# A decoder layer with a product-key FFN: maxima and indices of the next step taken in the middle of a step, and the gather of the indices moved to GpSimd

## The reference, cut to what matters

```python
q = jnp.einsum('bnd,de->bne', x, w_q)                      # 2 x 8 heads x 128
q = (q - mean) * rsqrt(var + BN_EPS) * bn_gamma + bn_beta  # over all 1600 tokens
sim = jnp.einsum('pbnhd,hkpd->pbnhk', q, keys)             # 2 halves x 8 heads x 32 keys
sx, ix = top_k(sim[0], 8);  sy, iy = top_k(sim[1], 8)
all_scores  = sx[..., :, None] + sy[..., None, :]          # 64 per head
all_indices = ix[..., :, None] * 32 + iy[..., None, :]
scores, pk = top_k(all_scores, 8)
indices = take_along_axis(all_indices, pk, axis=-1)        # 64 experts of 1024 per token
h = softmax(scores) * gelu_new(einsum('bnd,bnhkd->bnhk', x, down_embed[indices]))
out = einsum('bnhk,bnhkd->bnd', h, up_embed[indices])
```

## Time and profile before

| | before |
|---|---|
| median of three runs | 1294.25 us |
| the profiled execution | 1297.17 us |
| its span, first to last instruction | 1295.5 us |
| FFN, within that span | from about 1001 us to the end |
| VectorE busy over the span | 1139.7 us, 88% |
| GpSimd busy over the span | 622.4 us, 48% |
| mean granted TensorE clock | 0.91 of full speed |

### The profile page before, as it was taken

How to read it: one execution, slowest core, us unless ns; L and a number is a source line. 1 busy time by engine, 2 the same in 40 slices (tenths; PEclk the granted TensorE clock), 3 DMA queues, 4 the chain that set the end, 5 groups by cost and what they waited for, 6 DMA issues and landing times. The chain is left out here.

```text
span 1295.5 us, 32702 instructions
## 1 busy us (share of the span) xinstructions
PE 1163.4 (90%) x12758; PEld 908.5 (70%) x12762; DVE 1139.7 (88%) x2858; ACT 885.1 (68%) x1248; POOL 622.4 (48%) x520
## 2 busy tenths in 40 slices
PE   6969999999999999999999999999997748888878
PEld 4746777777767777776777777677776628778778
DVE  7768899999989999898999989998986679999984
ACT  4768888888888888888988888898874332222111
POOL 3226667757566775756677575767240300000000
PEclk9779999999999999999999999999998765667666
DMA  8119999999999999999999999998996300000000
GB/s 176 25 47 206 195 193 197 199 183 191 200 206 200 191 203 184 191 206 194 212 184 203 186 196 203 180 186 177 187 188 134 91 1 2 5 6 5 5 5 6
DMA packets 665393, 186.25 MB, mean 144 GB/s; under 512 B 653938, under 2 KB 662294, under 8 KB 664854
## 3 DMA queue, kind: packets, MB, share of 16 engines
q1 hardware_dynamic: 665238, 184.16, 74.7%
HBM read 19.97 MB, written 0.82 MB: 16 GB/s over the span
## 5 line engine op out<-in xcount | busy, mean ns | idle before, releaser
L1174 PE MATMUL ps<-pT,xa_hi 128*128 128x128 f16 x2288 | 380.8, 217 | 20.9 <-ACT uT L1009 20.9
L986 ACT ACTIVATE e<-ps,bias 128x1444 f32<-128x1444 f32 (+1 forms) x208 | 305.8, 1470 | 128.8 <-DVE bias L1058 128.1
L1178 PE MATMUL ps<-pT,xa_hi 128*128 128x128 f16 x2288 | 380.7, 217 | 2.2 <-DMA pT<-p 2.2
L1175 PE MATMUL ps<-pT,xa_lo 128*128 128x128 f16 x2288 | 380.8, 217 | 0.0
L1056 DVE TENSOR_REDUCE nmax<-ps 128x1 f32<-128x1444 f32 (+1 forms) x208 | 343.9, 1653 | 14.1 <-PE ps L1158 13.0
L1068 DVE TENSOR_TENSOR p<-e,p 128x1408 f16<-128x1408 f32 (+3 forms) x288 | 304.4, 1098 | 41.9 <-ACT p L994 41.0
L994 ACT ACTIVATE p<-e 128x1408 f16<-128x1408 f32 (+1 forms) x208 | 288.2, 1385 | 13.9 <-ACT e L986 0.7
L942 POOL TENSOR_TENSOR p<-e,p 128x1408 f16<-128x1408 f32 (+1 forms) x128 | 196.5, 1556 | 181.9 <-ACT p L994 181.9
L1174 PEld LDWEIGHTS ps<-pT,xa_hi 128*128 128x128 f16 x2288 | 222.1, 98 | 48.9 <-issue 36.0
L1156 PE MATMUL ps<-xT_hi,q_hi 128*128 128x512 f16 (+1 forms) x624 | 229.9, 368 | 4.0 <-POOL q_lo L931 3.3
L1175 PEld LDWEIGHTS ps<-pT,xa_lo 128*128 128x128 f16 x2288 | 222.1, 98 | 12.9
(11 more groups left out here) (238 smaller groups left out, 1929.2 us busy)
## 6 DMA issues: line engine op xcount, KB each, us to landing
raw<-in_ctx SPq DMA_DIRECT2D x16, 704.0 KB
pT<-p SPq DMA_TRANSPOSE x416, 3.7
f_wq<-in_L_ffn_w_q SPq DMA_DIRECT2D x1, 1024.0 KB, 5.3
f_wqt<-in_ffn_wq_t SPq DMA_DIRECT2D x2, 512.0 KB, 6.7
raw<-in_ctx SPq DMA_DIRECT2D x48, 18.0 KB
x_tok<-in_x SPq DMA_DIRECT2D x4, 200.0 KB
out_x<-ost SPq DMA_DIRECT2D x6, 128.0 KB, 1.9
wk_t<-in_wk_t SPq DMA_DIRECT2D x1, 512.0 KB, 8.7
```

The costliest lines, as they stand in the source:

```text
L986: act.activation(e32[t % E_BUF][rows, :], score_banks(t)[rows, 0:T], ACT.Exp, bias=bias[rows, t % N_BUF:t % N_BUF + 1]).then_inc(e_done, 1)
L1174: pe.matmul(out, hi, ph, start=n == 0, stop=False)
L1175: pe.matmul(out, lo, ph, start=False, stop=False)
L1178: pe.matmul(out, hi, pl, start=False, stop=False)
```

## The change

It touches only `ffn`.

- The gather's multiply and its three additions leave VectorE. A new function `gathered(i)` does them on GpSimd, with the semaphore `gather` between them. It waits for the mask (`pick`) and for `idxw` (`wide_idx`). VectorE waits for its result (`sel_done`) before `eu`.
- The maxima, the indices and the cast `idxf` of step i+1 are made during step i. All 32 maxima and `AHEAD` = 20 of the 32 `max_index` stand between `sel`'s weights (L1655) and `eu`. The other 12 and the cast stand behind L1674. `EARLY` and its six maxima go.
- `weigh(i - 1, 0)` and `weigh(i - 1, 1)` stood ahead of the maxima of `comb`, `weigh(i - 1, 2)` behind L1629. Now 0 is behind L1629, 1 behind L1655, 2 ahead of the wait for the gather, 3 behind `norm_shift`.
- The three parts of `norm_stats(i - 2)` stand among the maxima and indices of the next step, part 2 behind the 20 indices. `norm_shift(i - 2)` stands behind the cast.
- GpSimd's order in a step becomes `norm_rstd(i - 2)`, `gathered(i)`, `combine(i + 1)`.
- ScalarE's order becomes `picks(i)`, `hidden(i, 0)`, `sims_out(i + 1)`, the exponentials, `hidden(i, 1)`, `last_norm(i - 2)`, then `rT`, `cT`, `w_hi`.

The diff, cut to its core:

```diff
         @block.gpsimd
+            def gathered(i):
+                nh, w = step_shape(i)
+                na = nh * NB
+                pool.wait_ge(pick, 3 * i + 3)
+                pool.wait_ge(wide_idx, i + 1)
+                pool.tensor_tensor(out=eq[...], in0=eq[...], in1=idxw[...], op=ALU.mult).then_inc(gather, 1)
+                pool.wait_ge(gather, 3 * i + 1)
+                pool.tensor_tensor(out=half4[...], in0=eq[0:w, 0:na, 0:4, :], in1=eq[0:w, 0:na, 4:8, :], op=ALU.add).then_inc(gather, 1)
+                pool.wait_ge(gather, 3 * i + 2)
+                pool.tensor_tensor(out=half2[...], in0=half4[0:w, 0:na, 0:2, :], in1=half4[0:w, 0:na, 2:4, :], op=ALU.add).then_inc(gather, 1)
+                pool.wait_ge(gather, 3 * i + 3)
+                pool.tensor_tensor(out=ij[...], in0=half2[0:w, 0:na, 0, :], in1=half2[0:w, 0:na, 1, :],
+                                   op=ALU.add).then_inc(sel_done, 1)
+
+            combine(0)
+            wide_rows(1)
             for i in range(NSTEP):
-                combine(i)
-                if i == 0:
-                    wide_rows(1)
                 if i >= 2:
                     norm_rstd(i - 2)
+                gathered(i)
+                if i + 1 < NSTEP:
+                    combine(i + 1)
         @block.scalar
             for i in range(NSTEP):
+                picks(i)
                 hidden(i, 0)
-                if i >= 2:
-                    last_norm(i - 2)
-                hidden(i, 1)
-                picks(i)
                 if i + 1 < NSTEP:
                     sims_out(i + 1)
                 act.wait_ge(dsc_done, i + 1)
                 act.activation(esc[...], dsc[...], ACT.Exp).then_inc(esc_done, 1)
+                hidden(i, 1)
+                if i >= 2:
+                    last_norm(i - 2)
                 act.wait_ge(selT_ps, i + 1)
         @block.vector, in step(i), behind the weights sel[:, 2]
-                dve.wait_ge(pick, 7 * i + 5)
-                dve.tensor_tensor(out=half4[...], ...)
-                ...
+                if i:
+                    weigh(i - 1, 1)
+                if i >= 2:
+                    norm_stats(i - 2, 0)
+                if i + 1 < NSTEP:
+                    next_maxima(i + 1)
+                if i >= 2:
+                    norm_stats(i - 2, 1)
+                if i + 1 < NSTEP:
+                    next_indices(i + 1, 0)
+                if i >= 2:
+                    norm_stats(i - 2, 2)
+                if i:
+                    weigh(i - 1, 2)
                 dve.wait_ge(sel_done, 4 * i + 1)
                 ...
                 dve.tensor_copy(sel[0:w, 0:2, 0:nh, :], erc[0:w, :, 0:nh, :]).then_inc(sel_done, 1)
+                if i + 1 < NSTEP:
+                    next_indices(i + 1, 1)
+                    next_cast(i + 1)
+                if i >= 2:
+                    norm_shift(i - 2)
                 if i:
                     weigh(i - 1, 3)
```

More of the change, by code:

```diff
@@ L1193 @@
 NSTEP = -(-NT // STEP_TOK)
-EARLY = 6
+AHEAD = 20
 PAD = P + 4
@@ L1277, in ffn @@
         sim_ps, sim_done, top_done, comb_done, best_done = (sem(n) for n in ("sim_ps", "sim_done", "top_done", "comb_done", "best_done"))
+        idxf_done, gather = sem("idxf_done"), sem("gather")
         dsc_done, esc_done, pick, sel_done, selT_ps, selT_done = (sem(n) for n in ("dsc_done", "esc_done", "pick", "sel_done", "selT_ps", "selT_done"))
@@ L1367, in norm_rstd @@
                 pool.tensor_tensor(out=frs[0:w, 0:nh], in0=fve[0:w, 0:nh], in1=nhalf[0:w, 0:nh], op=ALU.pow).then_inc(z_rstd, 1)
+            def gathered(i):
[3 more added lines that the diff above has]
+                pool.wait_ge(wide_idx, i + 1)
+                pool.tensor_tensor(out=eq[0:w, 0:na, :, :], in0=eq[0:w, 0:na, :, :], in1=idxw[0:w, 0:na, :, :], op=ALU.mult).then_inc(gather, 1)
+                pool.wait_ge(gather, 3 * i + 1)
+                pool.tensor_tensor(out=half4[0:w, 0:na, :, :], in0=eq[0:w, 0:na, 0:4, :], in1=eq[0:w, 0:na, 4:8, :], op=ALU.add).then_inc(gather, 1)
+                pool.wait_ge(gather, 3 * i + 2)
+                pool.tensor_tensor(out=half2[0:w, 0:na, :, :], in0=half4[0:w, 0:na, 0:2, :], in1=half4[0:w, 0:na, 2:4, :], op=ALU.add).then_inc(gather, 1)
+                pool.wait_ge(gather, 3 * i + 3)
+                pool.tensor_tensor(out=ij[0:w, 0:nh, :, :].rearrange("s a n k -> s (a n) k"), in0=half2[0:w, 0:na, 0, :], in1=half2[0:w, 0:na, 1, :],
+                                   op=ALU.add).then_inc(sel_done, 1)
+            combine(0)
+            wide_rows(1)
             for i in range(NSTEP):
-                combine(i)
-                if i == 0:
-                    wide_rows(1)
                 if i >= 2:
                     norm_rstd(i - 2)
+                gathered(i)
+                if i + 1 < NSTEP:
+                    combine(i + 1)
             norm_rstd(NSTEP - 2)
@@ L1432, in picks @@
                 nh, w = step_shape(i)
-                act.wait_ge(pick, 7 * i + 1)
+                act.wait_ge(idxf_done, i + 1)
+                if i:
+                    act.wait_ge(gather, 3 * i - 2)
                 act.activation(idxw[0:w, 0:nh * NB, :, :],
@@ L1568, in norm_shift, with next_maxima, next_indices, next_cast @@
                                          op0=ALU.mult, op1=ALU.mult).then_inc(fnm_done, 1)
+            def next_maxima(i):
+                nh, w = step_shape(i)
+                if i:
+                    dve.wait_ge(sim_done, i)
+                    dve.wait_ge(comb_done, i)
+                    dve.wait_ge(top_done, 2 * i)
+                    dve.sem_inc(f_waited, 1)
+                for hf in range(nh):
+                    for n in range(NB):
+                        if not i and n % FH == 0 and hf == 0:
+                            dve.wait_ge(first_done, n // FH + 1)
+                            dve.sem_inc(f_waited, 1)
+                        ins = dve.max(top[0:w, hf, n, :], simb[0:w, hf, n, :])
+                ins.then_inc(top_done, 1)
+            def next_indices(i, part):
+                nh, w = step_shape(i)
+                if part == 0:
+                    dve.wait_ge(top_done, 2 * i + 1)
+                    dve.wait_ge(idxf_done, i)
+                    dve.sem_inc(f_waited, 1)
+                for k in range(*((0, min(AHEAD, nh * NB)), (min(AHEAD, nh * NB), nh * NB))[part]):
+                    hf, n = divmod(k, NB)
+                    ins = dve.max_index(idx[0:w, hf, n, :], top[0:w, hf, n, :], simb[0:w, hf, n, :])
+                    if k == nh * NB - 1:
+                        ins.then_inc(top_done, 1)
+            def next_cast(i):
+                nh, w = step_shape(i)
+                dve.wait_ge(top_done, 2 * i + 2)
+                dve.wait_ge(wide_idx, i)
+                dve.tensor_copy(idxf[0:w, 0:nh, :, :], idx[0:w, 0:nh, :, :]).then_inc(idxf_done, 1)
             def step(i):
@@ L1572, in step @@
                 j, na, nb = nh * HK, nh * NB, nh * NC
[L1573 to L1614, removed]
                 dve.wait_ge(comb_done, i + 1)
@@ L1631, in step @@
                 if i:
-                    weigh(i - 1, 2)
+                    weigh(i - 1, 0)
                 dve.wait_ge(best_done, 2 * i + 2)
@@ L1636, in step @@
                 dve.tensor_scalar(pij[0:w, 0:nh, 1, :], flat, K8 - 1, None, ALU.bitwise_and).then_inc(pick, 1)
-                dve.wait_ge(pick, 7 * i + 2)
+                dve.wait_ge(pick, 3 * i + 1)
                 dve.tensor_copy(pijf[0:w, 0:nh, :, :], pij[0:w, 0:nh, :, :]).then_inc(pick, 1)
@@ L1641, in step @@
                 dve.tensor_reduce(ssum[0:w, 0:nh, :], esc[0:w, 0:nh, :, :], AX_X, ALU.add).then_inc(soft_done, 1)
-                dve.wait_ge(pick, 7 * i + 3)
+                dve.wait_ge(pick, 3 * i + 2)
                 dve.tensor_tensor(out=eq[0:w, 0:na, :, :],
@@ L1648, in step @@
                 dve.reciprocal(srec[0:w, 0:nh, :], ssum[0:w, 0:nh, :]).then_inc(soft_done, 1)
-                dve.wait_ge(wide_idx, i + 1)
-                dve.wait_ge(pick, 7 * i + 4)
-                dve.tensor_tensor(out=eq[0:w, 0:na, :, :], in0=eq[0:w, 0:na, :, :], in1=idxw[0:w, 0:na, :, :], op=ALU.mult).then_inc(pick, 1)
                 dve.wait_ge(soft_done, 3 * i + 2)
@@ L1701, in step @@
                 ins.then_inc(oneh_done, 1)
+            next_maxima(0)
+            for part in range(2):
+                next_indices(0, part)
+            for k in range(1, NG):
+                centred(k)
+            dve.wait_ge(narrow_done, 1)
+            next_cast(0)
             for i in range(NSTEP):
```

## The result

The changed kernel takes 1325.84 us, the median of four runs (1322.06 to 1326.49); the kernel before, on the same chip, 1296.64 us. The ratio is 1.0214, with a 95% interval from 1.0192 to 1.0236: slower by about 28 us by the ratio, 29.2 between the medians. The span of the profiled execution is 1323.3 us, against 1295.5.

The account below looks back on a forecast made before the run. VectorE was taken to bound the kernel, busy 35.21 of 36.64 us a step. Step 0's 4.8 us and 4 x (5.6 + 2.0) make 35 us, on the median of 1294.25: 1329 us, range 1308 to 1336.

Parts of the forecast that it names:

- The gain on offer: On VectorE, from the gather's multiply to `eu` less `sel`: 2.65 us of a 36.5 us step can leave.
- The gather's price: On GpSimd, one multiply and three additions with semaphores between them take 8.2 us a step.
- the rival of a fast fp16: On GpSimd, the gather takes only 4.2 us, for a time of 1300 to 1310 us; chance 0.12.
- Where it starts: In steps 2 to 6 the gather waits behind `norm_rstd(i - 2)` until only 0.6 us of `weigh` cover it.
- A step of 2 to 4: Counted from the end of `mv_lo`: 42.1 us against 36.5, 5.6 us more, and 2.0 more for stalls.
- Stall (a): In steps 2 to 5 `combine(i + 1)` holds up `eu`, `erc` and the cast of `sel`: 2.0 us a step.
- Step 5: Counted as one of four equal steps, 2 to 5, each 5.6 + 2.0 us longer.
- Steps 0, 1, 6: Step 0 was to be 4.8 us longer, steps 1 and 6 unchanged.
- Stall (b): In steps 0 and 1 `sel` stands still beside GpSimd's 4.1 us multiply: 0 to 4 us each.
- The wait for the exponentials: In step 0, a 5.7 us wait shrinks as `hidden(0, 1)` no longer stands ahead: 4.3 us back.
- The case without stalls: The same wait for the gather, but VectorE's small operations not held up by GpSimd: 1316 us; chance 0.2.
- The case on the other side: The gather hides and TensorE limits a step to 34.2 us: faster, 1284 us; chance 0.03.

Follow-up runs that it names:

- the swap: The changed kernel with GpSimd running `gathered(i)` ahead of `norm_rstd(i - 2)`: 1305.64 us, ratio 1.0069.
- the last kernel: The changed kernel with gather ahead of norm, `sel` ahead of mask, `combine(i + 1)` after the cast of `sel`, `last_norm` behind `w_hi`: 1286.21 us, ratio 0.9924.

## Why the prediction was right, point by point

The time predicted was 1329 us, measured are 1325.8. Against the kernel before, 35 us had been expected; the spans show 27.8, the medians 29.2. That the time comes closer than the difference is luck: the 35 us were added to a median of 1294.25, and the kernel before, measured with the changed one, had 1296.64. The 2.4 us offset part of the error.

- *The gain on offer.* 2.65 us a step were to leave VectorE. Only where the wait and the stalls were gone was it to be had: 36.5 to 33.9 us. Of these 2.6 us the new order by itself gives 0.5 (35.98 with the gather on VectorE), the move to GpSimd the other 2.1.
- *The gather's price.* Forecast 4.08, 2.13, 1.16, 0.67 and 0.2 for the semaphores. Measured 4.08, 2.13, 1.14 and 0.67, 8.25 in all. The line drawn through the operations with an fp32 input held for fp16 alone, and the rival of a fast fp16 is out.
- *Where it starts.* `pow` behind `fve`, the multiply behind `pow`, in every step from 2 on. The forecast wait at `eu` was 8.3 us, the waits in steps 2 to 4 are 8.44, 8.25 and 8.22. In step 5 it is 6.11, since VectorE had first waited 2.27 us at `weigh` 2 for TensorE. That this is a matter of order was shown twice, by the swap and by the statistics placed first.
- *A step of 2 to 4.* 44.1 forecast, 43.6 measured. Stall (a) was set at 2.0 us between 0 and 2.1; it is 0.86 + 0.75 = 1.6, and taking `comb` away gave 1.5 to 1.8 back.
- *Step 5: the term that was wrong.* The sum took four equal steps, 4 x (5.6 + 2.0). But step 5 prepares step 6, which has 64 tokens and one half: 16 maxima and 16 indices instead of 32 each, no second part of the indices, and one `comb` instruction. Together that is some 16 x 0.10 + 16 x 0.16 + 0.75 = 4.9 us, and step 5 is 5.0 shorter than steps 2 to 4. It takes 38.68 us, 2.2 more than before and not 7.6. These 5.4 us are most of what the forecast was too high by; steps 2 to 4 add 1.4, step 0 0.8.
- *Steps 0, 1, 6.* Stall (b) came in full, 4.08 us in each of steps 0 and 1. But it hid other waits: taken away alone, it gave back 0.1 us in step 0 and 1.2 in step 1, since the gather's end and `comb` take its place. Step 0 is 4.0 longer (4.8 forecast), step 1 0.4 shorter (0), step 6 0.4 shorter (0). The wait for the exponentials fell from 5.7 to 0.5 us; 5.2 back in place of the 4.3 taken is the 0.8 that step 0 was forecast too long.
- *The case without stalls* (1316 us, chance 0.2) is out. The Trainium skill ("SBUF — State Buffer", section on the two separate sides) has it that whichever of the two engines comes first, GpSimd or a VectorE operation with two SBUF inputs or in a 2-port mode, holds the shared ports for its whole instruction. The traces agree where GpSimd came first: `sel`, with two inputs in SBUF, lasts as long as GpSimd's multiply (4.08 us beside 4.05), a `tensor_scalar` of 128 numbers up to the end of a `comb` instruction (0.97 in place of 0.23), while `max`, `max_index` and `weigh` with one input in PSUM pass. No line shown here has GpSimd held up by VectorE.
- *Busy time as a measure.* The case on the other side, a gather that hides, was a matter of 0.7 ns an element with that list. With the order mended it hides, but for 0.15 us, at 2.1 ns an element (8.25 us for 3840). That case set TensorE's limit of a step at 34.2 us; the last kernel shows 33.8.

## What to carry to other kernels

When work moves to an idle engine, follow its instruction list and not its busy share: the moved work starts when the instruction ahead of it has what it waits for, and here that was given by the very work meant to cover it. Beside GpSimd's two-input operations place what they can't hold up (here maxima, indices, a product with an input in PSUM), and keep the small operations of the main chain away from them, if need be by a wait. In a sum over steps look at what the last ones prepare, not only at what they do.

## What the runs showed of the hardware that was not expected

- That GpSimd's two-input operations on fp16 alone cost the same as with an fp32 input was taken on trust in the forecast; the runs now show it: 4.08 us for 2048 elements a partition and 2.13 for 1024, against 2.86 for 1408 with fp32.
- Two `comb` instructions without a gap between them (2.1 us) don't keep VectorE out altogether. With each of them it ends one of its small operations: `eu` 1.14 and the first `erc` 0.97 in one order, both `erc` 1.07 and 1.10 in another. The stall so costs 2.1 less the 0.5 us that these two take anyway, 1.6, where I had taken 2.0.
- Size is no protection: `fve`, a `tensor_scalar` of two numbers a partition, took 1.16 us in place of 0.14 beside a GpSimd addition (step 5 of the kernel with the gather and `sel` moved).
